# Four of the nine taps of the first stage's convolution computed on DVE instead of PE

## What is computed

```python
x = jax.lax.conv_general_dilated(sx, w_down, window_strides=(2, 2), padding=((1, 1), (1, 1)),
                                 feature_group_count=c2, dimension_numbers=('NCHW', 'OIHW', 'NCHW'))
xx = jax.lax.stop_gradient(x[0].reshape(c, h * w))   # image 0 alone goes into k-means
labels = _kmeans_labels(xs)                          # xs: xx normalised, 10 iterations
v5 = jnp.einsum('bchw,ck->bkhw', x, soh / ...)       # cluster means, every image
mu, var = _gmm_fit(wa)                               # mixture of two, 10 iterations, every image
y = jax.nn.sigmoid(...)                              # one gate per cluster
up = jnp.repeat(gate * x + x, 2, axis=1) * w_up
return _bilinear_up_x2(up) + sx                      # then layer 1 adds a shift per channel
```

## Time and profile before

| | |
|---|---|
| median of 3 runs | 2359.64 us |
| lowest, highest | 2356.22, 2361.98 us |
| the profiled execution's own time | 2354.2 us |
| its span, first to last instruction | 2352.4 us |
| mean granted TensorE clock | 0.864 |
| busy share: PE, DVE, ACT, POOL | 84%, 57%, 54%, 41% |
| stage 0, first matmul to the end of the last | 11.6 to 148.8 us |
| k-means, to the first mixture step | 149.6 to 317 us |

### The profile page before, as it was taken

The page is one execution under the profiler, slowest core; times in us unless marked ns, Lnnn a source line. Parts: engine busy times, 40 slices in busy tenths (PEclk is TensorE's granted clock), DMA queues, the critical chain, the costliest instruction groups (busy, mean ns, idle before and its releaser), DMA issues.

```text
span 2352.4 us, 37758 instructions
## 1 busy us (share of the span) xinstructions
PE 1974.8 (84%) x12185; PEld 1163.7 (49%) x12185; DVE 1345.7 (57%) x3488; ACT 1276.0 (54%) x1582; POOL 961.8 (41%) x1240
## 2 busy tenths in 40 slices
PE   7997679998999989999998999989999898445653
PEld 2336633444555455445554455445554555344543
DVE  0035244257665776476646765576657765777754
ACT  5533024366666665666566656665666655333653
POOL 0000001145454454445544454454544545445872
PEclk9997579999999999998999999898999998555766
DMA  6641045379999999999999999999999999876999
GB/s 240 247 176 71 0 185 208 145 300 402 407 362 422 425 425 381 411 405 405 387 395 424 425 417 394 401 398 403 366 422 425 425 372 376 331 272 251 417 427 405
DMA packets 109872, 808.80 MB, mean 344 GB/s; under 512 B 10880, under 2 KB 10880, under 8 KB 11392
## 3 DMA queue, kind: packets, MB, share of 16 engines
q1 hardware_dynamic: 75424, 542.35, 55.8%
q10 hardware_dynamic: 34272, 264.25, 28.7%
HBM read 538.12 MB, written 268.44 MB: 343 GB/s over the span
## 4 chain that ended last, share of the span: by engine, by line
PE 61%; DVE 18%; DMA 12%; DVEq 4%; issue 3%; ACT 1%; ACTq 0%; SPq 0%
PE ps L649 34%; PE ps L839 8%; PE ps L660 6%; DVE xres L1195 5%; PE ps L789 4%; DMA xres<-x 4%; PE ps L800 3%; DMA out<-xres 3%; DVEq L1198 2%; DMA xin<-x 2%; DVE part L866 2%; DMA out<-xin 2%; PE ps L826 1%; PE ps L705 1%; DVE xin L1195 1%
## 5 line engine op out<-in xcount | busy, mean ns | idle before, releaser
L649 PE MATMUL ps<-xin,taps 128*64 128x512 f32 (+1 forms) x4608 | 1082.9, 623 | 18.2 <-DMA xin<-x 14.6
L1195 DVE SCALAR_TENSOR_TENSOR xres<-ps,scale,xres 128x512 f32<-128x512 f32 x928 | 634.0, 745 | 131.3 <-PE ps L839 66.6
L649 PEld LDWEIGHTS ps<-xin,taps 128*64 128x64 f32 x4608 | 335.9, 137 | 683.2 <-issue 676.3
L586 ACT ACTIVATE xres<-xres,shift 128x2048 f32<-128x2048 f32 x232 | 455.5, 1993 | 118.3 <-DMA xres<-x 115.3
L567 ACT ACTIVATE junk<-xin 128x2048 bf16<-128x2048 f32 x256 | 488.8, 1909 | 32.3 <-issue 21.2
L839 PE MATMUL ps<-cst,pairs 64*128 64x128 f32 x4096 | 367.4, 348 | 107.6 <-DVE xres L1195 68.2
L839 PEld LDWEIGHTS ps<-cst,pairs 64*128 64x128 f32 x4096 | 335.6, 252 | 120.8 <-issue 115.9
L558 ACT ACTIVATE pairs<-ps 128x512 f32<-128x512 f32 x256 | 144.0, 594 | 388.5 <-PE ps L789 383.1
L489 POOL TENSOR_TENSOR lines<-lines,above 128x64 f32<-128x64 f32 x128 | 41.0, 320 | 642.9 <-DVEq L1078 374.3
L490 POOL TENSOR_TENSOR lines<-lines,conv 128x1024 f32<-128x1024 f32 x128 | 303.5, 2371 | 0.0
L485 POOL TENSOR_TENSOR lines<-rise,cst 128x1152 f32<-128x1152 f32 x128 | 271.3, 2120 | 23.8 <-issue 13.2
(11 more groups left out here) (170 smaller groups left out, 1434.0 us busy)
## 6 DMA issues: line engine op xcount, KB each, us to landing
xin<-x ACTq DMA_DIRECT2D x126, 2048.0 KB, 12.8
xres<-x SPq DMA_DIRECT2D x232, 1024.0 KB, 14.1
out<-xres SPq DMA_DIRECT2D x232, 1024.0 KB, 9.7
xin<-x SPq DMA_DIRECT2D x24, 1024.0 KB, 14.4
out<-xin SPq DMA_DIRECT2D x24, 1024.0 KB, 15.5
xin<-x SPq DMA_DIRECT2D x2, 2048.0 KB, 12.1
cst<-consts SPq DMA_DIRECT2D x1, 420.0 KB, 3.2
wg<-w_guide SPq DMA_DIRECT2D x1, 256.0 KB, 12.6
```

The source lines that it names most:

```text
L586: act.activation(c, c, ACT.Identity, bias=shift[:, p, 2 * t + i:2 * t + i + 1]) \
L649: mm = pe.matmul(half[:, :, 1:] if kx == 0 else half, taps[:, 2 * t + i, n, :], tap_input(h, i, ky, kx), start=n == 0, stop=n == len(TAPS) ...
L1195: m = dve.scalar_tensor_tensor(dst, up, sc, dst, ALU.mult, ALU.add)
```

## The change

In stage 0, DVE computes four of the nine taps, (1,2), (2,1), (2,2) and (0,1), for each block of input channels on its own: the first tap as a `tensor_scalar` (input times the channel's weight), the other three as `scalar_tensor_tensor` (input times weight, plus what is there), into 512 contiguous floats a partition of the unused `xres` (`tap_part`). That is eight instructions of 128x512 a step, with a drain after every two. PE does the other five taps as before, then waits for DVE (`dve_taps`) and adds DVE's two sums with one more pair of matmuls, whose weights are the plain 0/1 pairing matrix. In addition ACT issues the next load ahead of its copy from PSUM, in stage 0 alone (`if not do_em`). Stages 1 to 9 are as before.

```diff
+TAPS_DVE = [(1, 2), (2, 1), (2, 2), (0, 1)]
...
+        def tap_part(h, i):
+
+            return xres[:, h, i, 0:CN // W, :].rearrange("c r w -> c (r w)")
...
                         act.wait_ge(conv_ps, g + 1)
+                        if not do_em:
+                            load_next(g, h, nxt)
                         act.activation(conv[:, p, ds(t * PX + CN * (2 * u + h), CN)],
...
                         act.drain().then_inc(conv_done, 1)
-                        if nxt is not None:
-                            nb, nt, nu = nxt
-                            act.wait_ge(halo, g + 2)
-                            load(act, j + nb, nt, 2 * nu + h, h)
+                        if do_em:
+                            load_next(g, h, nxt)
...
+                shared = isinstance(j, int) and j == 0
...
+                    if shared and (ky, kx) in TAPS_DVE:
+                        continue
...
+                if shared:
+                    pe.wait_ge(dve_taps, g + 1)
+                    for i in range(2):
+                        mm = pe.matmul(acc[G * i:G * (i + 1)].rearrange("c r w -> c (r w)"), cst[:, C_SEL:C_SEL + G],
+                                       tap_part(h, i), start=False, stop=True)
...
+            def shared_taps(t, s):
+
+                h = s % 2
+                g = S * t + s
+                dve.wait_ge(x_in[h], 8 * (S * t + s - h) + 16)
+                if g >= 2:
+                    dve.wait_ge(conv_ps, g - 1)
+                for n, (ky, kx) in enumerate(TAPS_DVE):
+                    if ky == 0:
+                        dve.wait_ge(halo, g + 1)
+                    for i in range(2):
+                        kt = 2 * t + i
+                        part_ = tap_part(h, i).rearrange("c (r w) -> c r w", w=WC)
+                        k = 3 * ky + kx
+                        if n == 0:
+                            dve.tensor_scalar(part_, tap_input(h, i, ky, kx), wd[:, kt, k:k + 1], None, ALU.mult)
+                        else:
+                            dve.scalar_tensor_tensor(part_, tap_input(h, i, ky, kx), wd[:, kt, k:k + 1], part_,
+                                                     ALU.mult, ALU.add)
+                    d = dve.drain()
+                d.then_inc(dve_taps, 1)
...
+            for t in range(TILES):
+                for s in range(S):
+                    shared_taps(t, s)
             dve.wait_ge(conv_done, STEPS)
```

More of the change, by code:

```diff
@@ L227, in build @@
         conv_ps = sem("conv_ps")
+        dve_taps = sem("dve_taps")
         conv_taken = sem("conv_taken")
@@ L596, in step, with load_next @@
                         act.drain().then_inc(conv_done, 1)
-                        if nxt is not None:
-                            nb, nt, nu = nxt
-                            act.wait_ge(halo, g + 2)
-                            load(act, j + nb, nt, 2 * nu + h, h)
+                        if do_em:
+                            load_next(g, h, nxt)
+                def load_next(g, h, nxt):
+                    if nxt is not None:
+                        nb, nt, nu = nxt
+                        act.wait_ge(halo, g + 2)
+                        load(act, j + nb, nt, 2 * nu + h, h)
                 def following(t, u):
@@ L649, in conv_taps @@
                         mm = pe.matmul(half[:, :, 1:] if kx == 0 else half, taps[:, 2 * t + i, n, :],
-                                       tap_input(h, i, ky, kx), start=n == 0, stop=n == len(TAPS) - 1)
+                                       tap_input(h, i, ky, kx), start=n == 0, stop=n == len(TAPS) - 1 and not shared)
+                if shared:
[3 more added lines that the diff above has]
+                                       tap_part(h, i), start=False, stop=True)
                 mm.then_inc(conv_ps, 1)
```

## The result

The changed kernel took 2335.63 us, the median of four runs (2334.59 to 2337.26). The kernel before took 2358.98 us, the median of four runs beside it. The ratio is 0.9901, with a 95% interval of 0.9884 to 0.9919: faster by 1.0%. The forecast was 2339.5 us, in a range of 2329 to 2352.

What follows compares the result with a forecast made beforehand. Two close limits bound stage 0: a load slot's 17.0 us cycle and PE's 16.6. A 17.2 us gain gave 2337.0 us against the profiled execution, 2342.4 on the median; forecast between them 2339.5, range 2329 to 2352.

Steps and rivals of the forecast that it cites:

- the sum: Stage 0's steps added up: its end moves from 148.8 to 130.8 us, less 0.85 us, a gain of 17.2 us.
- PE's end to the issue: Stage 0, PE's last record to the next load's issue: 1.25 us falls to 0.56 with the load ahead of ACT's copy.
- landing to start: Stage 0, from a load's landing to the start of work on it: 0.24 us, as PE took before.
- D: DVE's eight instructions in a step of stage 0: 5.95 us; each 0.1 us is worth 0.9 us of the total.
- The drain: Stage 0 on DVE: a drain after every two instructions costs 0.19 us, three of them inside a step.
- The rival of the strided read: DVE's taps read every second column at 0.36 us more each, total 8.5 us up; chance 0.08 slower, 0.06 near no change.
- POOL's lock: Stage 0: POOL's halo copy may hold DVE up 0.40 us a step; charged at nothing, kept for the range.
- Loads: Rival in stage 0: the two slots' loads overlap by 1.25 us and slow each other, gain 8.8 to 8.4 us smaller; chance 0.08.
- The clock: Rival in stage 0: PE's waits drop its granted clock to half, stage end 41 us up; chance 0.03.
- The stage's end: Stage 0: step 14 closes at 124.8 us, step 15 one DVE part later at 130.8, where it was 148.8.
- The late copy: End of stage 0: ACT's copy from PSUM, now behind the load's issue, delays DVE once, by 0.85 us.
- the slack at the transposes: Start of k-means: PE still waits 1.9 us for DVE before its transposes, 3.42 before, so stage 0's gain lasts.

Runs made afterwards that it cites:

- multiply-add experiment: The changed kernel with DVE's first tap as scalar_tensor_tensor plus a tile of zeros instead of tensor_scalar: 2339.71 us, ratio 0.9916 to the kernel before.
- taps-only kernel: The changed kernel with ACT's load behind its copy again, DVE keeping its four taps: 2353.32 us, ratio 0.9969 to the kernel before.
- the repeat: The changed kernel run once more, unedited, for the scatter between executions: 2333.90 us, ratio 0.9901 to the kernel before.

## Why the prediction was right

The mechanism was the one forecast, and the forecast lay 3.9 us above the result, inside the range. That the two numbers came so close is in part luck: the sum gave stage 0 a gain of 17.2 us, and it was 24.0. Most terms of its cycle were a little too dear, step by step:

| term of the cycle | predicted, us | measured, us |
|---|---|---|
| PE's end to the issue | 0.56 | 0.25 |
| load | 7.2 | 7.16 |
| landing to start | 0.24 | 0.02 |
| D, eight instructions on DVE | 5.95 | 5.50 |
| handover and closing pair | 1.20 | 1.18 |
| the cycle | 15.15 | 14.10 |

- **DVE's part, the largest miss.** The two `tensor_scalar` were priced at 745 ns, "the higher price because the shape is the same". They take 0.49 us and start 0.40 us apart: the shape was the same, the operation wasn't. The multiply-add experiment gives the difference as 0.53 us in D. The Trainium skill (VectorE: DVE Perf Modes, The perf-mode tier table), cited in the prediction, has `tensor_scalar` at twice the rate of a two-tensor operation; the estimate from it, some 0.5 us less, was the better price, though the ratio of the two durations here is 0.65 (487 to 750 ns) and not a half.
- **The drain, the scalar_tensor_tensor and the strided read** were right: six in 4.39 us. The rival of the strided read falls: 750 ns as the median, 5 more than in the earlier trace rows.
- **POOL's lock** was charged at nothing, with 0.40 us a step kept for the range. In the trace of the change, the timeline of POOL and that of DVE:

```profile
40.61 0.62 POOL L446 COPY xin<-xin 128x256 f32<-128x256 f32 x1 [6.91 <-DMA xin<-x]
47.40 0.40 POOL L446 COPY xin<-xin 128x256 f32<-128x256 f32 x1 [6.17 <-PE ps L669]
```

```profile
40.48 1.02 DVE L929 TENSOR_SCALAR xres<-xin,wd 128x512 f32<-128x512 f32 x2 [2.58 <-DMA xin<-x]
41.58 4.40 DVE L931 SCALAR_TENSOR_TENSOR xres<-xin,wd,xres 128x512 f32<-128x512 f32 x6
46.58 0.88 DVE L929 TENSOR_SCALAR xres<-xin,wd 128x512 f32<-128x512 f32 x2 [0.61 <-DMA xin<-x]
```

  In one slot the copy starts in the middle of DVE's first pair: the pair takes 0.14 us more than in the other slot, the copy 0.22 more. So the two do hold each other up, but POOL pays more of it, and DVE loses 0.14 us there, not 0.40. In the other slot its six multiply-adds took 4.39 to 4.53 us, so it lost no more than that there. The rule that the prediction cites from the Trainium skill (SBUF — State Buffer, Who interferes with whom) speaks of DVE operations with two SBUF inputs; in the multiply-add kernel the first pair has two, and took 1.55 us against 1.41, its copy 0.88. That agrees with the rule in kind; the estimate of 0.40 us in most steps was too high.
- **The issue** comes 0.25 us behind PE's end. The prediction had taken 0.60 and 0.09 off the 1.25 between end and issue. Another 0.31 went with the copy that moved away, most of it the copy's start and the second drain behind it (0.11 and 0.15 in the chain of before). The taps-only kernel, with the copy in between again, takes 1.20.
- **Landing to start**: the 0.24 us were PE's. DVE, which now follows a landing on the path, starts after 0.02.
- **Loads** overlap without cost at two slots: 7.16 and 7.18 us. That rival falls.
- **The clock** was given a chance of 0.03 for a fall in most cycles. It fell once in the stage, at PE's five taps from 82.99; earlier, after a longer stop, it had held:

```profile
26.56 4.72 PE L664 MATMUL ps<-xin,taps 128*64 128x512 f32 x20 [2.36 <-DMA xin<-x]
...
82.99 6.31 PE L664 MATMUL ps<-xin,taps 128*64 128x512 f32 x20 [2.05 <-ACTq L603]
```

  The 6.31 us are more than DVE's 5.5 and so lay on the path. In the taps-only kernel, with idle stretches of 3.35 us, the fall came in many cycles. The rival was nearer than its chance said.
- **The stage's end.** Step 0 closed at 18.8 us, as in the sum (12.8 + 5.95), but for another reason: PE's own five taps took 6.35 us there, longer than DVE's part. Seven cycles of 1.05 us less are 7.4 us. The one with the slow clock took 14.83 (82.78 to 97.61), which gives 0.7 back, and step 14 closed at 118.5 us, for 124.8 forecast. Step 15 was to land before DVE is free; it landed 0.48 us after, and still closed only 5.8 us behind step 14, for 5.95. The last closing pair ended at 124.3 where 130.8 was forecast. The late copy cost less than the 0.85 charged: by the chains, from PE's end to the reduction are 1.56 us (124.33 to 125.89), before 1.13 (148.78 to 149.91). So the reduction came at 125.89, not 132.7, and the slack at the transposes was 2.37 us, for a forecast of 1.9.
- **The total.** The gain at the stage's end was 24.0 us for 17.2 forecast. In the profiled execution 4.5 us were lost again in stages 2 to 7, which the repeat shows to be scatter; between the medians 23.4 are left (2358.98 - 2335.63). On the median of before, the sum gave 2342.4, 6.8 us too much. The forecast of 2339.5 is nearer only because it was put between that and the 2337.0 from the profiled execution, which lay below the median.

## What to carry to other kernels

A stage with two buffers has a cycle: issue, load, the longest consumer, what must follow it, and again the issue. Write that sum down beside each engine's own work. Where the two are close, an edit to either alone can give little and both together more (here 3.6 and 10.3 us against 24.0, by the estimate above, more than half of the gap being the clock that fell in the longer waits of the taps-only kernel). Once the consumers are faster than the cycle, a third buffer is the next step: it brought 21 us more, and moved the bound back to the engines and the DMA together. Price an instruction by its own operation, not by a neighbour of the same shape.

## What I had not expected

- The granted clock in one program differed between executions with the same busy time of PE (1.64 us of 4 in both) and the same stop before it (2.36 us): once 1.00 throughout, once 0.50 after it. A change that makes PE wait must allow for that.
- The 2 MB loads reach 370 to 377 GB/s with three slots, though each takes 9.3 us, and DVE and PE keep their speed beside it (754 ns; 4.67 us for 20 records).
- Stages 2 to 7, with the same instructions, took 1478.3 to 1492.0 us over these kernels, and 1479.2 and 1485.3 in two executions of one.
